# A decoder layer on one core: the ends of cross attention and of the fourth pass put in another order

## The chip, the cores and the metric

The kernel runs on one core of a Trainium2 chip. The metric is the device time of one execution in microseconds (us). A core has five engines with a program each: TensorE (PE; its weight loads are listed as PEld), VectorE (DVE), ScalarE (ACT), GpSimd (POOL) and SyncE (SP, which issues most transfers). Each runs its instructions in program order and waits on semaphores for the others.

## The reference

A decoder layer on 32 sequences of 128 rows and 128 features, in three residual parts, each on layer-normalised rows:

```python
x = x + _L0_attn_ref(_layernorm(x), W_qkv)                  # causal, one head
x = x + _L0_xattn_ref(_layernorm(x), ctx, ctx, mask, ...)   # 16 heads of 8
x = x + _L0_ffn_ref(_layernorm(x), w_gate, w_up, w_down)

def act_qdq(x):                                             # in _L0_ffn_ref
    scale = max(max(abs(x)) / 32767, 1e-12)                 # one maximum over the whole tensor
    return clip(round(x / scale), -32768, 32767) * scale
x = act_qdq(x)
up = act_qdq(x @ dequant(w_up).T)
gate = act_qdq(x @ dequant(w_gate).T)
sig = fixed_qdq_u16(sigmoid(gate))
gate = act_qdq(gate * sig)
o = act_qdq(gate * up)
return o @ dequant(w_down).T
```

Each `act_qdq` needs the largest absolute value of its whole tensor before any element can be rounded, so the feed-forward part is a row of passes over all 32 sequences with a common maximum between them.

## The kernel before

The 32 sequences (`B`) lie in eight groups (`NG`) of four (`GB`), so a group is `GT` = 512 columns wide; the hidden layer of a group has three such pieces, `FW` = 3 x `GT` = 1536 columns, and `PB` = 768 is its half. All engines' programs are written out by hand in one block each; semaphores carry the order between them, and a wait names a semaphore and the count that must be reached.

**Cross attention** runs sequence by sequence. For sequence n PE multiplies the probabilities with the values (`pv`, two halves), ScalarE copies the result out (`out_copy`), PE turns it (`queries`), VectorE divides by the sums (`attend(n)`: a reciprocal and a product), PE turns the quotient (`turn(n)`), ScalarE copies it (`turn_copy`) and PE projects it (`project(n)`). For the last three sequences VectorE adds the projection to the row (`residual`) and takes statistics (`stat3`); `aggregate3_last` closes the statistics of one or two sequences of the last group, GpSimd makes the factor of them (`roots3_last`, lines 556 to 569) and normalises two of its four sequences (line 566), VectorE the other two (`row3_last`). `largest3` takes the largest absolute value of normalised rows. PE turns the normalised rows group by group (`turn_early_rows3`, `turn_rows3`, line 630), and ScalarE or VectorE copies them (`rows3_copy`; VectorE has only group 2, line 1703). VectorE's own order at the end stands in lines 1739 to 1762, PE's in lines 948 to 985.

**The passes of the feed-forward part.** The gate (first), the up product's maximum (second), gate times sigmoid (third), and gate times up (fourth) each go over the eight groups; then the last pass multiplies by the down weights (line 1059). At the close of a pass VectorE spreads the largest value over a 128 x 128 tile (`mxw`), PE turns it (`over_partitions`, line 976), and VectorE takes the maximum over the partitions and its reciprocal (`levels_from`): the rounding of the next pass needs these.

In the **fourth pass** PE recomputes the up product of group g into PSUM (line 989), ScalarE rounds it to integers, partly into SBUF (`up_levels`, line 1344) and partly in place in PSUM (`up_levels_in_place`, line 1349), and rounds the other factor (`silu_levels`, line 1355). The product of the two is shared: GpSimd makes the first `product_split(g)` columns (lines 586 to 598) and VectorE the others (`product`, line 1891), and VectorE takes the maximum of the whole (`product_largest`, line 1820). Semaphores: `c_tn` counts the rounded gates, `c_un` the rounded ups, `c_op` GpSimd's products, `c_od` VectorE's, `c_mx` the maxima. PE fills the wait before the closing transposition with products that nobody reads (`idle_products`, line 971; two instructions each), each lot released by one of these counts (line 1049).

Of the kernel before, what the change touches and what calls it, by code (L numbers as in the profile page):

```python
# [39 lines left out]
B = 32  # L40
# [25 lines left out]
def decoder(nc, x, ctx_in, mask, Wqkv, Wq, bq, Wk, bk, Wv, bv, Wo, bo, w_gate, w_up, w_down, out):  # L66
    with ExitStack() as ctx:
# [129 lines left out]

        def product_split(g):

            return PB if g < UW or g == NG - 2 else 2 * GT  # L200

        def up_made(g):

            return g + 1 if g < UW else 2 * g - UW + 2
# [162 lines left out]
        def _(pool):  # L367
# [218 lines left out]
            for g in range(NG - 1):  # L586
# [3 lines left out]
                if g < UW:  # L590
# [2 lines left out]
                                        ).then_inc(S["c_op"], 1)  # L593
            g = NG - 1
            pool.wait_ge(S["c_tn"], NG + 1)
            pool.wait_ge(S["c_un"], up_made(NG - 2) + 2)
            nc.gpsimd.tensor_tensor(GI[:, g * FW:g * FW + GT], tn[:, g % 2, 0:GT], un[g % 3][:, 0:GT], ALU.mult
                                    ).then_inc(S["c_op"], 1)


        @block.tensor
        def _(pe):
# [176 lines left out]
            def turn(n):  # L779
                pe.wait_ge(S["t_o"], n + 1)  # L780
                pe.transpose(bank(6 + n % 2)[:, 0:P], on_[:, :], ident[:, :]).then_inc(S["t_oT"], 1)  # L781
# [167 lines left out]
                cross(n)  # L949

            queries(B - 1)
            for g in range(3):
                turn_early_rows3(g)
            turn(B - 1)
            pe.wait_ge(S["u_tca"], 1)
            turn_weights3(0, 0)
            project(B - 1)
# [88 lines left out]
                    over_partitions(4, 1)  # L1046

            pe.wait_ge(S["g_lev"], 4)
            for name, value, k in (("c_tn", NG, 6), ("c_tn", NG + 1, 4), ("c_op", NG - 1, 4), ("c_op", NG, 4), ("c_od", NG + 1, 6)):
                pe.wait_ge(S[name], value)  # L1050
                idle_products(1, k)
            over_partitions(5, 0)
# [35 lines left out]
        def _(act):  # L1088
# [251 lines left out]
            def up_levels(g, part):  # L1340
                act.wait_ge(S["c_u"], g + 1)
                wait(act, "c_op", g - 2)
                wait(act, "c_od", g - 2)
                act.activation(un[g % 3][:, part], up_bank(g)[:, part], ACT.Copy, scale=lev[:, 2:3]
                               ).then_inc(S["c_un"], 1)

            def up_levels_in_place(g, part):
                act.wait_ge(S["c_u"], g + 1)
                act.activation(up_bank(g).bitcast(I32)[:, part], up_bank(g)[:, part], ACT.Copy, scale=lev[:, 2:3]
                               ).then_inc(S["c_un"], 1)  # L1350
# [23 lines left out]
                silu_levels(g, slice(0, FW))  # L1374
            silu_levels(NG - 1, slice(0, FW))
            up_levels_in_place(NG - 1, slice(2 * GT, FW))
            up_levels(NG - 1, slice(0, GT))
            up_levels_in_place(NG - 1, slice(GT, 2 * GT))


            act.wait_ge(S["g_lev"], 5)
# [18 lines left out]
        def _(dve):  # L1400
# [256 lines left out]
            def attend(n):  # L1657
                dve.wait_ge(S["t_tr"], n + 1)
                wait(dve, "t_o", n)
                o3 = bank(6 + n % 2)[:, 2 * P:4 * P].rearrange("p (h c) -> p h c", c=VW)  # L1660
                V.reciprocal(orec[:, :], o3[:, :, DK]).then_inc(S["t_rec"], 1)
                dve.wait_ge(S["t_rec"], n + 1)
                wait(dve, "t_oT", n)
                V.tensor_tensor(on_[:, :].rearrange("p (h e) -> p h e", e=DK), o3[:, :, 0:DK],
                                bc(orec[:, :].unsqueeze(2), [P, H, DK]), ALU.mult).then_inc(S["t_o"], 1)

            def residual(n):
                dve.wait_ge(S["t_wo"], n + 1)
                x = X[:, n * P:(n + 1) * P]
                V.tensor_tensor(x, bank(6 + n % 2)[:, P:2 * P], x, ALU.add).then_inc(S["t_xd"], 1)  # L1670
# [4 lines left out]
            def stat3(n):  # L1675
                b = n % GB
                if n < B - TAIL:
                    dve.wait_ge(S["t_x2"], n + 1)
                else:
                    dve.wait_ge(S["t_xd"], n + 1 - (B - TAIL))  # L1680
                V.bn_stats(stats3(n // GB)[:, b, :], X[:, n * P:(n + 1) * P]).then_inc(S["u_stat"], 1)
# [8 lines left out]
            def aggregate3_last(b0, b1):  # L1690
                dve.wait_ge(S["u_stat"], GB * (NG - 1) + b1)
                for b in range(b0, b1):
                    m = V.bn_aggr(norms[1]["mvar"][:, 2 * b:2 * b + 2], stats3(NG - 1)[:, b, :])
                m.then_inc(S["u_agg"], 1)
# [25 lines left out]
            for n in range(B - 1):  # L1720
                g, b = divmod(n, GB)
                if n > 0:
                    attend(n - 1)
                if g > 1 and b > 1:
                    k = b - 2
                    dve.wait_ge(S["u_x3"], GB * (g - 2) + 2 * k + 2)
                    largest3(g - 2, 2 * (g - 2) + k, (2 * k, 2 * k + 2))
                if n + 3 < B:
                    maxima(n + 3, 0)
                if 1 < n < B - 1:  # L1730
                    stat3(n - 2)
                if g > 0 and b == 1:
                    aggregate3(g - 1)
                if n + 3 < B:
                    maxima(n + 3, 1)
                if n == B - 2:
                    residual(n - 1)
                    stat3(n - 1)
            aggregate3_last(0, 2)
            dve.wait_ge(S["u_x3"], GB * (NG - 2))  # L1740
            largest3(NG - 3, 2 * NG - 5, (2, 4))
            attend(B - 2)
            dve.wait_ge(S["u_x3"], GB * (NG - 1))
            largest3(NG - 2, 2 * NG - 4, (0, GB))
            residual(B - 2)
            stat3(B - 2)
            aggregate3_last(2, 3)
            attend(B - 1)
            rows3_copy(2, 2)
            dve.wait_ge(S["u_x3"], GB * (NG - 1) + 2)  # L1750
            largest3(NG - 1, 2 * NG - 3, (0, 2))
# [143 lines left out]
                largest(4, col, GI[:, g * FW + c.start:g * FW + c.stop], "c_mx")  # L1895

            for g in range(NG - 1):
                dve.wait_ge(S["c_un"], up_made(g) - (g >= UW))
                dve.wait_ge(S["c_tn"], g + 1 + (g > 0))
                product(g, slice(product_split(g), FW))  # L1900
                if g == 0:
                    V.tensor_tensor(unit[:, 4:5], scale[:, 3:4], scale[:, 2:3], ALU.mult).then_inc(S["g_unit"], 1)
                    guard_of(4)
                if g > 0:
                    dve.wait_ge(S["c_op"], g)
                    dve.wait_ge(S["c_od"], g)
                    product_largest(g - 1, g - 1, slice(0, FW))
            g = NG - 1
            dve.wait_ge(S["c_od"], NG - 1)
            product_largest(g - 1, g - 1, slice(PB, FW))  # L1910
            dve.wait_ge(S["c_op"], NG - 1)
            product_largest(g - 1, g, slice(0, PB))
            dve.wait_ge(S["c_tn"], NG + 1)
            for k, c in enumerate((slice(2 * GT, FW), slice(GT, 2 * GT))):
                dve.wait_ge(S["c_un"], up_made(NG - 2) + 1 + 2 * k)
                product(g, c)
            dve.wait_ge(S["c_op"], NG)
            dve.wait_ge(S["c_od"], NG + 1)
            product_largest(g, g + 1, slice(0, FW))
            dve.wait_ge(S["c_mx"], NG + 1)  # L1920
            dve.wait_ge(S["g_guard"], 8)
            largest_of(4, 2 * NG)
            dve.wait_ge(S["g_early"], 8)
# [72 lines left out]
```

## Time and profile before

| what | value |
|---|---|
| time before, median of three runs | 332.85 us (332.31 to 333.15) |
| profiled execution, its own time | 332.82 us |
| its span, first to last instruction | 331.0 us |
| mean granted TensorE clock | 0.995 of full speed |
| PE busy | 304.9 us, 92% |
| VectorE busy | 273.5 us, 83% |
| ScalarE busy | 255.1 us, 77% |
| GpSimd busy | 192.1 us, 58% |

All profile times are from the start of the span. The end of cross attention lies at 203 to 213 us, the end of the fourth pass at 293 to 304 us, and the last pass after it. Busy shares are averages over stages with different limits; they say nothing of either place by themselves. A line of the timeline gives start, duration, engine, source line, operation, result and operands with their shapes, the count of merged instructions, and in brackets the idle time of the engine before it and what ended that.

### The profile page before, as it was taken

How to read it: one execution, taken by the hardware profiler on the slowest of the kernel's cores; microseconds unless marked ns; L12 is line 12 of the kernel's file. 1: busy time of each engine (PE TensorE's matmuls, PEld its weight loads, DVE VectorE, ACT ScalarE, POOL GpSimd, SP SyncE). 2: the span in 40 equal slices, each digit the busy share in tenths (PEclk: the TensorE clock that was granted, in tenths of full speed). 3: DMA queues.
4: the chain of work that ended last, by engine and by line, in shares of the span. 5: the costliest groups of instructions: out<-in, count | busy, mean ns of one | idle time of the engine just before them, and what ended most of it. 6: DMA issues, size and time to landing. Idle time of an engine off the chain costs nothing.

```text
span 331.0 us, 9933 instructions
## 1 busy us (share of the span) xinstructions
PE 304.9 (92%) x3741; PEld 208.7 (63%) x3741; DVE 273.5 (83%) x652; ACT 255.1 (77%) x470; POOL 192.1 (58%) x339
## 2 busy tenths in 40 slices
PE   2899999999999999999999999999978689697996
PEld 1587877877656666666666665854423244357996
DVE  5349998878979999999999984877789996989754
ACT  3258988887789989989988987787797768993940
POOL 3467999984238698768658578200067773781000
PEclk9999999999999999999999999999997999999999
DMA  6891336672011556500000000000000000000134
GB/s 155 248 300 35 96 110 184 190 219 95 30 42 49 176 160 191 170 4 5 3 5 2 4 5 2 1 0 0 2 0 0 1 1 2 0 0 1 34 95 128
DMA packets 23755, 22.70 MB, mean 69 GB/s; under 512 B 3546, under 2 KB 21403, under 8 KB 23579
## 3 DMA queue, kind: packets, MB, share of 16 engines
q1 hardware_dynamic: 22170, 21.78, 21.4%
q8 instruction: 30, 0.49, 0.6%
q10 hardware_dynamic: 1536, 0.28, 0.5%
q14 instruction: 19, 0.15, 0.1%
HBM read 15.75 MB, written 6.31 MB: 67 GB/s over the span
## 4 chain that ended last, share of the span: by engine, by line
PE 65%; DVE 12%; ACT 8%; POOL 7%; issue 4%; DMA 2%; SPq 1%; POOLq 0%; ACTq 0%; DVEq 0%
PE banks L763 11%; PE banks L707 9%; PE banks L989 8%; DVE mxs L1820 7%; PE banks L1059 7%; PE banks L637 5%; PE banks L785 4%; PE banks L776 3%; PE banks L630 3%; ACT ng L1355 2%; PE banks L781 2%; PE banks L716 2%; POOL rstd L380 2%; PE banks L649 2%; PE banks L971 2%
## 5 line engine op out<-in xcount | busy, mean ns | idle before, releaser
L1594 DVE TENSOR_REDUCE nm<-banks 128x4 f32<-128x512 f32 x128 | 83.1, 682 | 7.2 <-PE banks L707 5.8
L1258 ACT ACTIVATE PT<-banks,bmask,vmask 128x1024 f32<-128x1024 f32 x64 | 76.6, 1199 | 0.0
L989 PE MATMUL banks<-X3T,upT 128*128 128x512 f32 x96 | 45.9, 620 | 9.9 <-DVE mxs L1820 7.3
L576 POOL TENSOR_TENSOR G<-ng,sq 128x1536 int32<-128x1536 int32 (+3 forms) x10 | 27.9, 2790 | 36.4 <-DVE sq L1851 36.4
L1820 DVE TENSOR_REDUCE mxs<-G 128x1 f32<-128x1536 int32 (+3 forms) x30 | 42.2, 1425 | 4.3 <-ACT G L1316 3.8
L763 PE MATMUL banks<-PT,VP 128*32 128x128 f32 x1024 | 41.2, 279 | 0.0
L989 PEld LDWEIGHTS banks<-X3T,upT 128*128 128x128 f32 x96 | 17.7, 196 | 33.8 <-issue 16.3
L707 PE MATMUL banks<-kd,qd 32*128 32x128 f16 x512 | 37.9, 217 | 1.1 <-ACT pT L1130 0.7
L1100 ACT ACTIVATE h<-X,shift,rstd 128x128 f32<-128x128 f32 x64 | 26.3, 483 | 10.2 <-POOL shift L425 10.1
L707 PEld LDWEIGHTS banks<-kd,qd 32*128 32x128 f16 x512 | 22.7, 92 | 17.7 <-DVE nm L1594 7.2
L763 PEld LDWEIGHTS banks<-PT,VP 128*32 128x32 f32 x1024 | 24.1, 109 | 9.8 <-issue 3.0
L380 POOL TENSOR_TENSOR rstd<-vare,mhalf 128x4 f32<-128x4 f32 (+2 forms) x26 | 25.3, 974 | 0.8
L711 PE MATMUL banks<-qd,kd 32*128 32x128 f16 x512 | 25.3, 217 | 0.1
L716 PE MATMUL banks<-mT,inj 32*128 32x128 bf16 x512 | 25.0, 215 | 0.0
L467 POOL CAST NM<-nm 128x64 bf16<-128x64 f32 x32 | 7.6, 237 | 28.8 <-DVE nm L1594 28.8
L482 POOL TENSOR_SCALAR X<-X,mvar,rstd 128x128 f32<-128x128 f32 x28 | 22.0, 793 | 0.0
L1059 PE MATMUL banks<-downT,sig 128*128 128x128 f32 x192 | 21.8, 276 | 0.0
L1059 PEld LDWEIGHTS banks<-downT,sig 128*128 128x128 f32 x192 | 21.6, 192 | 0.1
L1242 ACT ACTIVATE oT<-banks 128x128 f32<-128x128 f32 x32 | 8.9, 277 | 12.4 <-PE banks L781 12.4
L1327 ACT ACTIVATE ng<-G,lev 128x1536 int32<-128x1536 f32 (+2 forms) x9 | 12.9, 1430 | 7.0 <-POOL G L576 5.9
L989 PE MATMUL banks<-X3T,gateT 128*128 128x512 f32 x42 | 18.2, 592 | 0.0
L1316 ACT ACTIVATE G<-banks 128x512 f32<-128x512 f32 x24 | 14.0, 596 | 4.6 <-PE banks L989 3.4
(200 smaller groups left out, 744.4 us busy)
## 6 DMA issues: line engine op xcount, KB each, us to landing
kd<-k_dram SPq DMA_DIRECT2D x32, 128.0 KB, 2.7
qd<-q_dram SPq DMA_DIRECT2D x32, 128.0 KB, 2.8
ctxg<-in_ctx_dram SPq DMA_DIRECT2D x8, 256.0 KB, 3.1
X3T<-m_dram SPq DMA_DIRECT2D x1, 1792.0 KB, 10.2
out_dram<-y SPq DMA_DIRECT2D x7, 256.0 KB, 2.3
X<-in_x_dram SPq DMA_DIRECT2D x3, 512.0 KB, 10.0
k_dram<-khi SPq DMA_DIRECT2D x7, 128.0 KB, 1.9
k_dram<-klo SPq DMA_DIRECT2D x7, 128.0 KB, 1.9
```

The lines of the kernel that those rows point to most:

```text
L380: nc.gpsimd.tensor_tensor(norms[k]["rstd"][:, c], norms[k]["vare"][:, c], mhalf[:, c], ALU.pow).then_inc(S[done], 1)
L576: nc.gpsimd.tensor_tensor(GI[:, c], ng[:, u, part], sq[:, u, part], ALU.mult).then_inc(S["b_t"], 1)
L707: return pe.matmul(bank(j % 2)[:, s * P:(s + 1) * P], qd[rows(j), n // GB, s, n % GB, :], kd[rows(j), n // GB, s, n % GB, :], start=True, ...
L711: pe.matmul(bank(2 + j)[:, s * P:(s + 1) * P], kd[rows(j), n // GB, s, n % GB, :], qd[rows(j), n // GB, s, n % GB, :], start=(s == 0), sto ...
L716: return pe.matmul(bank(2 + j)[:, s * P:(s + 1) * P], inj[rows(j), s, :], mT[rows(j), n % 2, :], start=False, stop=True, skip_group_check= ...
L763: m = pe.matmul(bank(6 + n % 2)[RT * s:RT * s + RT, a * P:(a + 1) * P], VP[:, n % 2, JT * s + 2 * a + k, :], PT[:, a, (NSET * k + s) * P:( ...
L989: m = pe.matmul(bank(2 + FC * (g % 2) + k), w[:, k * P:k * P + P], grp(X3T, g), start=True, stop=True)
L1059: m = pe.matmul(bank(n)[:, b * P:(b + 1) * P], on[:, u, c * GT + b * P:c * GT + b * P + P], downT[:, c * P:(c + 1) * P], start=(c == 0), s ...
L1100: act.activation(dst[:, b_ * P:(b_ + 1) * P], seq(X, g, b_), ACT.Identity, scale=norms[k]["rstd"][:, b_:b_ + 1], bias=norms[k]["shift"][:, ...
L1258: act.activation(PT[:, a, :], bank(2 + 2 * a, 2), ACT.Exp, bias=bmask[:, n:n + 1], scale=vmask[:, n:n + 1]).then_inc(S["t_exp"], 1)
L1594: V.tensor_reduce(nm[:, n % 2, c:c + NSET], bank(u).rearrange("p (h m) -> p h m", m=P), AX.X, ALU.max, negate=True).then_inc(S["t_max"], 1)
L1820: V.tensor_reduce(mxs[:, k, col:col + 1], src, AX.X, ALU.max, apply_absolute_value=True).then_inc(S[done], 1)
```

## The change

Two places are edited together.

In the fourth pass `product_split` gives GpSimd two thirds (1024 columns) of group 6 (`NG - 2`) instead of half. Of group 7 GpSimd makes two thirds, each in an instruction of its own, where it made the first third; the second third's up levels therefore go to SBUF (`up_levels`) instead of in place. VectorE makes only the last third. VectorE's list becomes: the maximum of group 5 ahead of its product of group 6, then that product, the maximum of its third, its product of group 7, the maximum of GpSimd's two thirds of group 6, and three maxima, one for each third of group 7. PE's idle products get one more release, six after the last product of GpSimd.

In the end of cross attention VectorE scales the output of sequence 30 ahead of the aggregate of sequences 28 and 29 and two maxima, and the output of sequence 31 ahead of the statistics and the aggregate of sequence 30. PE turns the rows of group 2 after the output of sequence 31 instead of before it.

```diff
--- before.py
+++ after.py
@@ -197,7 +197,7 @@
 
         def product_split(g):
 
-            return PB if g < UW or g == NG - 2 else 2 * GT
+            return PB if g < UW else 2 * GT
 
         def up_made(g):
 
@@ -593,9 +593,10 @@
                                         ).then_inc(S["c_op"], 1)
             g = NG - 1
             pool.wait_ge(S["c_tn"], NG + 1)
-            pool.wait_ge(S["c_un"], up_made(NG - 2) + 2)
-            nc.gpsimd.tensor_tensor(GI[:, g * FW:g * FW + GT], tn[:, g % 2, 0:GT], un[g % 3][:, 0:GT], ALU.mult
-                                    ).then_inc(S["c_op"], 1)
+            for k in range(2):
+                pool.wait_ge(S["c_un"], up_made(NG - 2) + 2 + k)
+                nc.gpsimd.tensor_tensor(GI[:, g * FW + k * GT:g * FW + (k + 1) * GT], tn[:, g % 2, k * GT:(k + 1) * GT],
+                                        un[g % 3][:, k * GT:(k + 1) * GT], ALU.mult).then_inc(S["c_op"], 1)
 
 
         @block.tensor
@@ -949,9 +950,10 @@
                 cross(n)
 
             queries(B - 1)
-            for g in range(3):
+            for g in range(2):
                 turn_early_rows3(g)
             turn(B - 1)
+            turn_early_rows3(2)
             pe.wait_ge(S["u_tca"], 1)
             turn_weights3(0, 0)
             project(B - 1)
@@ -1046,7 +1048,7 @@
                     over_partitions(4, 1)
 
             pe.wait_ge(S["g_lev"], 4)
-            for name, value, k in (("c_tn", NG, 6), ("c_tn", NG + 1, 4), ("c_op", NG - 1, 4), ("c_op", NG, 4), ("c_od", NG + 1, 6)):
+            for name, value, k in (("c_tn", NG, 6), ("c_tn", NG + 1, 4), ("c_op", NG - 1, 4), ("c_od", NG, 4), ("c_op", NG, 4), ("c_op", NG + 1, 6)):
                 pe.wait_ge(S[name], value)
                 idle_products(1, k)
             over_partitions(5, 0)
@@ -1374,8 +1376,8 @@
                 silu_levels(g, slice(0, FW))
             silu_levels(NG - 1, slice(0, FW))
             up_levels_in_place(NG - 1, slice(2 * GT, FW))
-            up_levels(NG - 1, slice(0, GT))
-            up_levels_in_place(NG - 1, slice(GT, 2 * GT))
+            for k in range(2):
+                up_levels(NG - 1, slice(k * GT, (k + 1) * GT))
 
 
             act.wait_ge(S["g_lev"], 5)
@@ -1736,16 +1738,16 @@
                 if n == B - 2:
                     residual(n - 1)
                     stat3(n - 1)
+            attend(B - 2)
             aggregate3_last(0, 2)
             dve.wait_ge(S["u_x3"], GB * (NG - 2))
             largest3(NG - 3, 2 * NG - 5, (2, 4))
-            attend(B - 2)
             dve.wait_ge(S["u_x3"], GB * (NG - 1))
             largest3(NG - 2, 2 * NG - 4, (0, GB))
             residual(B - 2)
+            attend(B - 1)
             stat3(B - 2)
             aggregate3_last(2, 3)
-            attend(B - 1)
             rows3_copy(2, 2)
             dve.wait_ge(S["u_x3"], GB * (NG - 1) + 2)
             largest3(NG - 1, 2 * NG - 3, (0, 2))
@@ -1895,29 +1897,34 @@
                 largest(4, col, GI[:, g * FW + c.start:g * FW + c.stop], "c_mx")
 
             for g in range(NG - 1):
+                if g == NG - 2:
+                    dve.wait_ge(S["c_op"], g)
+                    dve.wait_ge(S["c_od"], g)
+                    product_largest(g - 1, g - 1, slice(0, FW))
                 dve.wait_ge(S["c_un"], up_made(g) - (g >= UW))
                 dve.wait_ge(S["c_tn"], g + 1 + (g > 0))
                 product(g, slice(product_split(g), FW))
                 if g == 0:
                     V.tensor_tensor(unit[:, 4:5], scale[:, 3:4], scale[:, 2:3], ALU.mult).then_inc(S["g_unit"], 1)
                     guard_of(4)
-                if g > 0:
+                if 0 < g < NG - 2:
                     dve.wait_ge(S["c_op"], g)
                     dve.wait_ge(S["c_od"], g)
                     product_largest(g - 1, g - 1, slice(0, FW))
             g = NG - 1
             dve.wait_ge(S["c_od"], NG - 1)
-            product_largest(g - 1, g - 1, slice(PB, FW))
+            product_largest(g - 1, g - 1, slice(2 * GT, FW))
+            dve.wait_ge(S["c_tn"], NG + 1)
+            dve.wait_ge(S["c_un"], up_made(NG - 2) + 1)
+            product(g, slice(2 * GT, FW))
             dve.wait_ge(S["c_op"], NG - 1)
-            product_largest(g - 1, g, slice(0, PB))
-            dve.wait_ge(S["c_tn"], NG + 1)
-            for k, c in enumerate((slice(2 * GT, FW), slice(GT, 2 * GT))):
-                dve.wait_ge(S["c_un"], up_made(NG - 2) + 1 + 2 * k)
-                product(g, c)
-            dve.wait_ge(S["c_op"], NG)
-            dve.wait_ge(S["c_od"], NG + 1)
-            product_largest(g, g + 1, slice(0, FW))
-            dve.wait_ge(S["c_mx"], NG + 1)
+            product_largest(g - 1, g, slice(0, 2 * GT))
+            dve.wait_ge(S["c_od"], NG)
+            product_largest(g, g + 1, slice(2 * GT, FW))
+            for k in range(2):
+                dve.wait_ge(S["c_op"], NG + k)
+                product_largest(g, g + 2 + k, slice(k * GT, (k + 1) * GT))
+            dve.wait_ge(S["c_mx"], NG + 3)
             dve.wait_ge(S["g_guard"], 8)
             largest_of(4, 2 * NG)
             dve.wait_ge(S["g_early"], 8)
```

## Rows read from the trace of the kernel before

**Rows 1.** Chain of work that ended last: start, us, what; the two closing transpositions.

```profile
212.78 0.30 PE banks L976
...
304.20 0.33 PE banks L976
```

**Rows 2.** Timeline of VectorE, end of cross attention.

```profile
204.26 0.29 DVE L1681 BATCH_NORM_STATS2 stats<-X 128x6 f32<-128x128 f32 x1
...
205.06 0.25 DVE L1661 RECIPROCAL orec<-banks 128x16 f32<-128x16 f32 x1
205.34 0.29 DVE L1664 TENSOR_TENSOR on_<-banks,orec 128x128 f32<-128x128 f32 x1
...
207.80 0.24 DVE L1661 RECIPROCAL orec<-banks 128x16 f32<-128x16 f32 x1
...
208.88 0.69 DVE L1703 COPY X3T<-banks 128x512 f32<-128x512 f32 x1 [0.52 <-PE banks L630]
...
209.84 0.29 DVE L1670 TENSOR_TENSOR X<-banks,X 128x128 f32<-128x128 f32 x1
```

**Rows 3.** Timeline of PE, the same stretch.

```profile
204.18 0.41 PE L776 MATMUL banks<-ident,oun 128*128 128x128 f32 x2 [0.28 <-ACT oun L1237]
...
205.69 0.33 PE L781 MATMUL banks<-ident,on_ 128*128 128x128 f32 x1 [0.52 <-DVE on_ L1664]
...
207.10 0.44 PE L776 MATMUL banks<-ident,oun 128*128 128x128 f32 x2
207.37 1.47 PE L630 MATMUL banks<-ident,X 128*128 128x128 f32 x12
208.68 0.27 PE L781 MATMUL banks<-ident,on_ 128*128 128x128 f32 x1
...
209.32 0.49 PE L785 MATMUL banks<-WXT,oT 128*128 128x128 f32 x2
```

**Rows 4.** Timeline of GpSimd, the same stretch: two sequences of group 7 normalised.

```profile
206.03 1.57 POOL L566 TENSOR_SCALAR X<-X,mvar,rstd 128x128 f32<-128x128 f32 x2
```

**Rows 5.** Timeline of VectorE, end of the fourth pass.

```profile
293.85 1.75 DVE L1820 TENSOR_REDUCE mxs<-G 128x1 f32<-128x1536 int32 x1
296.29 0.95 DVE L1891 TENSOR_TENSOR G<-ng,banks 128x768 int32<-128x768 int32 x1 [0.70 <-ACT ng L1355]
...
300.54 1.28 DVE L1891 TENSOR_TENSOR G<-ng,banks 128x512 int32<-128x512 int32 x2
301.92 1.75 DVE L1820 TENSOR_REDUCE mxs<-G 128x1 f32<-128x1536 int32 x1
```

**Rows 6.** Timeline of GpSimd and ScalarE, end of the fourth pass.

```profile
293.22 2.37 POOL L592 TENSOR_TENSOR G<-ng,unx 128x1024 int32<-128x1024 int32 x1 [0.33 <-ACT ng L1355]
...
296.26 1.82 POOL L592 TENSOR_TENSOR G<-ng,X 128x768 int32<-128x768 int32 x1 [0.67 <-ACT ng L1355]
...
298.66 0.70 ACT L1349 ACTIVATE banks<-banks,lev 128x512 int32<-128x512 f32 x1
298.95 1.27 POOL L597 TENSOR_TENSOR G<-ng,X 128x512 int32<-128x512 int32 x1 [0.86 <-ACT X L1344]
```

**Rows 7.** VectorE's groups by line and shape: count, busy us, mean ns, idle before.

```profile
L1820 DVE TENSOR_REDUCE mxs<-G 128x1 f32<-128x512 f32 x6 | 3.8, 677 | 0.2 <-ACT G L1316 0.2
...
L1891 DVE TENSOR_TENSOR G<-ng,banks 128x512 int32<-128x512 int32 x5 | 3.3, 682 | 0.7 <-ACT ng L1355 0.7
L1891 DVE TENSOR_TENSOR G<-ng,X 128x768 int32<-128x768 int32 x2 | 2.5, 1228 | 2.4 <-ACT ng L1355 2.4
```

**Rows 8.** Timeline of PE, the last idle products before the transposition at 304.20.

```profile
301.88 1.60 PE L971 MATMUL banks<-ident 128*128 128x128 f32 x12 [0.45 <-DVE G L1891]
```

**Rows 9.** Timeline of PE in the third pass, and one stretch's busy times with granted clock.

```profile
241.98 5.42 PE L989 MATMUL banks<-X3T,upT 128*128 128x512 f32 x12 [0.84 <-DVE mxs L1820]
249.47 7.23 PE L989 MATMUL banks<-X3T,upT 128*128 128x512 f32 x12 [2.07 <-DVE mxs L1820]
...
251.00:252.00 1.00, 1.00 (x2) 0.34 (x1) 1.00 (x1) 0.97 (x2) 1.00 (x1) 0.50 0.00 0
```

## The prediction, made before the change was run

> **What bounds the kernel now.** I read the profile from the outside in. The chain of waits comes first, because it names the work that ended last. Its steps at the two edited places are VectorE and PE work, and each place closes with a transposition on PE that gathers one maximum over the partitions: at 212.78 for the levels of the normalised rows, and at 304.20 for the levels of the product [rows 1]. Nothing of the next pass can begin before its transposition, so time saved ahead of one is saved for the whole kernel, and time saved beside it is lost. The question at each place is therefore when the transposition's input is ready.
>
> Then I read the timeline of each engine ahead of both points, since shares of the span say nothing of a place 8 us long. In the end of cross attention the reader is to see that VectorE does statistics and maxima that nobody waits for yet, while PE waits for the scaled output of sequence 30: the product starts at 205.34 and PE's transposition only at 205.69, though the input (two transpositions of 0.41 from 204.18) was ready at 204.59 [rows 2, 3]. In the end of the fourth pass the reader is to see VectorE idle for 0.70 before 296.29, waiting for ScalarE, and then never idle until 303.67 [rows 5]; GpSimd ends its last product at 298.95 + 1.27 = 300.22 and does nothing more [rows 6]. So VectorE alone sets this end.
>
> **The change, part 1: the end of the fourth pass.** Counted from 295.6, VectorE's list is rebuilt. Group 7's middle third goes to GpSimd, and so does a sixth of group 6; the whole maximum of group 5 moves ahead of group 6's product, into the idle 0.70. One reduce more is issued in all: eight instructions where there were seven.
>
> Steps between starts: two independent 512-wide products with an operand in PSUM take 1.28 together, at a mean of 0.682 each, so an instruction that waits for nothing starts 0.08 before its predecessor ends [rows 5, 7]. One that waits for its predecessor's own result starts 0.10 after it (300.54 + 1.28 = 301.82, then 301.92) [rows 5]. A reduce of 512 costs 0.677 [rows 7], one of 1536 costs 1.75 [rows 5]; 1024 lies half way, an estimate of 1.21.
>
> The maximum of group 5 needs GpSimd's product of group 5, done at 293.22 + 2.37 = 295.59 [rows 6], and VectorE, free at 293.85 + 1.75 = 295.60 [rows 5]. With 0.04 for the signal it starts at 295.64. Then: group 6's third at 297.31; its maximum, which waits for it, at 298.09; group 7's third at 298.69; the maximum of group 6's two thirds at 299.29; group 7's three maxima at 300.42, 301.02 and 301.62. From the start of the last reduce to the transposition it was 304.20 - 301.92 = 2.28 with 1536 wide [rows 1, 5]; with 512 it is 2.28 - (1.75 - 0.68) = 1.21. VectorE is ready for the transposition at 302.83, a gain of 1.37.
>
> The others must keep up. GpSimd: group 6 now takes 2.37 instead of 1.82, so 296.26 to 298.63, still before the 298.95 at which ScalarE's levels let group 7 begin [rows 6]; nothing is queued late. The second third of group 7 needs ScalarE's last levels, done at 298.66 + 0.70 = 299.36 [rows 6], and follows at 300.22, done at 301.49. The last reduce at 301.62 is thus only 0.1 behind it. ScalarE: group 6's levels change from 768 + 768 to 512 + 1024 columns, and the last 512 go to SBUF instead of PSUM; equal width, and I cost it at nothing. It hides under GpSimd's 1.27, and if it ran late by more than 0.86 it would show.
>
> PE is the third that must keep up. Its idle products before the transposition are in program order, and the last six now wait for GpSimd's last product. In the trace the six are twelve instructions of 1.60 in all [rows 8]; a successor overlaps such a run by 0.16 (208.84 against 208.68) [rows 3], so the transposition comes about 1.44 behind their start, or nearer 1.34 if no gap lies ahead of them. From 301.54 this gives 302.9 to 303.0. PE's own fillers, not VectorE, are then last, by about 0.1. I take 302.9: a gain of **1.3**. Bounds: 1.4 (VectorE gates) and 0.6 (the GpSimd rival below).
>
> **Part 2: the end of cross attention.** Scaling output 30 moves ahead of an aggregate and two maxima; VectorE is free at 204.26 + 0.29 = 204.55 [rows 2]. The reciprocal starts when its input is done, at 204.62 instead of 205.06; the product follows 0.28 later, as in the trace, and everything behind it on PE and ScalarE up to the transposition of output 31 comes 0.43 earlier: PE's transposition at 205.26, the two of output 31 at 206.67 instead of 207.10, done at 207.11 [rows 3]. Output 31 is now scaled ahead of the statistics of 30: reciprocal at 207.14 instead of 207.80 [rows 2], product done at 207.71.
>
> PE in the meantime turns eight blocks of rows from 206.94, 0.109 each [rows 3], and is free at 207.81, just when the scaled output arrives (207.77). It is turned at 207.81 instead of 208.68. The four blocks of group 2, moved behind it, end at about 208.52 instead of 208.84 [rows 3]; VectorE's copy of them, which waited 0.52 for PE, starts at 208.56 instead of 208.88 [rows 2]. From there VectorE's list to the transposition at 212.78 is unchanged and almost without a gap, and what it needs is there: the last projection is ready for VectorE at 209.2 (ScalarE's copies come earlier by the same shift) where VectorE reaches it at 209.52; before, these two tied (209.32 + 0.49 = 209.81 against a start at 209.84) [rows 2, 3]. The gain is **0.32**. The moved statistics reach GpSimd later, the first of them by about what scaling output 30 takes, 0.53 with its step; its rows of group 7 end at 206.03 + 1.57 + 0.53 = 208.13 instead of 207.60 [rows 4], a microsecond before their maximum at 209.17, so I cost this at nothing. If that cover were gone, up to the whole 0.32 would be. Bounds: 0, and 0.43, the whole shift ahead of the copy.
>
> **The sum.** The profiled execution took 332.82, its span 331.0 and 1.8 around it, and agrees with the median of 332.85. 332.82 - 1.3 - 0.32 = **331.2**.
>
> **The rivals.**
> *Cross attention gives nothing.* GpSimd's later factors, or PE's reordered turns, end as late as before. For it: many signals from engine to engine lie in 4 us, and PE and the scaled output tie at 207.8. Against it: the margins above. Time: 332.82 - 1.3 = 331.5.
>
> *GpSimd becomes the bound of the fourth pass.* Its last product runs at 1.27 only in one row, alone against VectorE's reduces. A VectorE product with both operands in SBUF took 1.23 on average beside GpSimd's products, against 0.95 for the one with an operand in PSUM [rows 5, 7]: sharing exists. If both of GpSimd's last products stretched by 1.23/0.95 = 1.29, they would end at 298.95 + 2 x 1.64 = 302.23, PE's transposition would come at 303.6, and the gain would be 0.6: 331.9. Against it: VectorE's new instructions beside them are reduces and products with an operand in PSUM, and GpSimd's 2.37 at 293.22 lies beside just these [rows 5, 6]. The Trainium skill, page GPSIMD Engine Reference, section Specifications, says the same: contention arises with VectorE instructions that have two SBUF inputs or use a two-port mode. By that rule the stretch would be nil and this case vanishes; the trace agrees as far as it goes, so its chance is small.
>
> *Slower: PE's clock falls.* Twelve matmuls of the third pass took 7.23 at 249.47 against 5.42 at 241.98; PE had been idle for 2.07 before, and the granted clock in 251 to 252 is 0.50, the lower level of 1.2 GHz [rows 9]. One such fall in the last pass, which is PE's, costs 1.8 and turns the forecast into 332.82 - 1.62 + 1.8 = 333.0, slower than before; it decides from a fall of 1.6 on. For it: the stretch ahead is idle products, whose times all move. Against it: their gaps shrink, the six new ones fill the hole that lay behind GpSimd's last product, and a stretch with 0.45 of idle ahead of the last fillers [rows 8] kept its clock. The Trainium skill, page TensorE: Matmul & The Clock Gate, section Part 1, says that the throttled state is the default and that activity releases it; by that rule fewer idle moments can only help, which the two rows of the third pass bear out.
>
> **How the numbers follow.** Forecast 0.70, nothing from cross attention 0.12, GpSimd bound 0.09, clock 0.04, others 0.05. Runs of this kernel spread by 0.3% (1.0 us), which is also what a measurement can tell from no change, so faster means below 331.85. Of the forecast 0.95 lies there, of the second case 0.8, of the third 0.45: together 0.80. Slower by over 0.3% is half of the clock case and a part of the others: 0.03; the rest, 0.17, is no difference. The range goes from both upper bounds, 332.82 - 1.42 - 0.43 = 331.0 less half the spread, 330.5, to the GpSimd case with some of the spread, 332.3.
>
> **What would show it.** In the changed profile: group 5's maximum on VectorE at 295.6 less 0.3, with no idle before the product of group 6; the last reduce 512 wide and within 0.2 of the end of GpSimd's last product; PE's fillers running into the last transposition; the copy of group 2's turned rows 0.3 earlier. I am wrong if VectorE waits for GpSimd ahead of one of its last two reduces by more than 0.2, if the 212.78 transposition has not moved, or if the last pass shows a granted clock below 1.

## The result, and the profile after

The changed kernel takes 330.55 us (median of 7 runs, 329.86 to 331.62) against 332.63 for the kernel before in the same comparison (332.07 to 333.28, 7 runs). The ratio is 0.9945 with a 95% interval of 0.9932 to 0.9958, so 1.4 to 2.3 us faster. The difference of the two medians, 2.08, lies in that interval. The profiled execution took 331.25 with a span of 329.5; against the profiled 332.82 of before that is 1.57 less.

Two stretches measure the two parts by themselves, free of whatever moved ahead of them. For cross attention it runs from the start of VectorE's addition of sequence 29's projection (the operation of `residual`) to the closing transposition; for the fourth pass from the start of ScalarE's rounding of group 6's gate (`silu_levels`) to the closing transposition.

| stretch, us | before | after | gain |
|---|---|---|---|
| end of cross attention | 212.78 - 203.94 = 8.84 | 212.51 - 204.00 = 8.51 | 0.33 |
| between the two | 294.59 - 212.78 = 81.81 | 294.33 - 212.51 = 81.82 | 0 |
| end of the fourth pass | 304.20 - 294.59 = 9.61 | 302.69 - 294.33 = 8.36 | 1.25 |

The lines that the table rests on, beside those of [rows 1]: first the three of before, then the four of after. The last line of each is VectorE's reading of the second transposition.

```profile
203.94 0.29 DVE L1670 TENSOR_TENSOR X<-banks,X 128x128 f32<-128x128 f32 x1 [1.82 <-PE banks L785]
294.59 3.06 ACT L1355 ACTIVATE ng<-G,lev 128x1536 int32<-128x1536 int32 x2
304.57 0.29 DVE L1773 TENSOR_REDUCE step<-banks 128x1 f32<-128x128 f32 x1 [0.42 <-PE banks L976]
...
204.00 0.29 DVE L1672 TENSOR_TENSOR X<-banks,X 128x128 f32<-128x128 f32 x1 [1.82 <-PE banks L786]
212.51 0.30 PE L978 MATMUL banks<-ident,mxw 128*128 128x128 f32 x1 [0.94 <-DVE mxw L1769]
294.33 3.06 ACT L1357 ACTIVATE ng<-G,lev 128x1536 int32<-128x1536 int32 x2
303.00 0.29 DVE L1775 TENSOR_REDUCE step<-banks 128x1 f32<-128x128 f32 x1 [0.59 <-PE banks L978]
```

Counted to that reading, the fourth pass gains a little more than to the start of the transposition: 304.57 - 294.59 = 9.98 before and 303.00 - 294.33 = 8.67 after, so 1.31. The transposition takes 0.33 after a wait [rows 1] and 0.27 right behind other matmuls, as below.

The timeline of VectorE in the end of the fourth pass, after (start, duration, engine, line, operation, operands, count):

```profile
293.59 3.53 DVE L1822 TENSOR_REDUCE mxs<-G 128x1 f32<-128x1536 int32 x2
297.04 0.68 DVE L1893 TENSOR_TENSOR G<-ng,banks 128x512 int32<-128x512 int32 x1
297.75 0.69 DVE L1822 TENSOR_REDUCE mxs<-G 128x1 f32<-128x512 int32 x1
298.35 0.68 DVE L1893 TENSOR_TENSOR G<-ng,banks 128x512 int32<-128x512 int32 x1
298.95 2.99 DVE L1822 TENSOR_REDUCE mxs<-G 128x1 f32<-128x1024 int32 x4
301.97 0.17 DVE L1712 TENSOR_REDUCE mx<-mxs 128x1 f32<-128x16 f32 x1
302.18 0.23 DVE L1931 TENSOR_SCALAR mxw<-mx 128x128 f32<-128x128 f32 x1
```

Where [rows 5] had 0.70 of idle time and a product of 768, no idle time is shown any more: the two maxima of 1536 run into each other, the product of 512 follows, and the last four maxima form one block. The spread maximum is ready at 302.18 + 0.23 = 302.41. PE and GpSimd in the same stretch:

```profile
296.07 6.78 PE L973 MATMUL banks<-ident 128*128 128x128 f32 x56 [0.59 <-ACT ng L1357]
302.69 0.27 PE L978 MATMUL banks<-ident,mxw 128*128 128x128 f32 x1
302.80 2.17 PE L973 MATMUL banks<-ident 128*128 128x128 f32 x18
...
296.00 2.36 POOL L592 TENSOR_TENSOR G<-ng,X 128x1024 int32<-128x1024 int32 x1 [0.67 <-ACT ng L1357]
298.69 2.51 POOL L598 TENSOR_TENSOR G<-ng,X 128x512 int32<-128x512 int32 x2 [0.32 <-ACT X L1346]
```

PE's 56 idle instructions stand in one row without a wait up to the transposition, which carries no idle time and no releaser and comes 0.28 after its input was made. That it waited for PE's own queue is tested below. Before, the idle products were over at 301.88 + 1.60 = 303.48 [rows 8], well ahead of the transposition at 304.20 [rows 1]. GpSimd ends at 298.69 + 2.51 = 301.20. VectorE's last maximum, one of 0.68 that ends with its block at 301.94, starts at about 301.26, only 0.06 later, so GpSimd is the next to become last.

The end of cross attention after, VectorE first and then PE, to be read against [rows 2, 3]:

```profile
204.69 0.26 DVE L1663 RECIPROCAL orec<-banks 128x16 f32<-128x16 f32 x1
204.98 0.29 DVE L1666 TENSOR_TENSOR on_<-banks,orec 128x128 f32<-128x128 f32 x1
...
208.66 0.69 DVE L1705 COPY X3T<-banks 128x512 f32<-128x512 f32 x1 [0.45 <-PE banks L631]
209.26 0.41 DVE L1708 TENSOR_REDUCE mxs<-X 128x1 f32<-128x256 f32 x1
...
205.33 0.33 PE L782 MATMUL banks<-ident,on_ 128*128 128x128 f32 x1
...
207.88 0.30 PE L782 MATMUL banks<-ident,on_ 128*128 128x128 f32 x1
208.02 0.60 PE L631 MATMUL banks<-ident,X 128*128 128x128 f32 x4
...
208.78 0.39 PE L786 MATMUL banks<-WXT,oT 128*128 128x128 f32 x2
```

The whole stretch lies 0.06 later in this execution. Output 30 is turned at 205.33 without a wait shown (0.52 before), output 31 at 207.88 instead of 208.68, and VectorE's copy starts at 208.66 instead of 208.88.

### The profile page after: what moved, and what is told of

Its sections match the earlier page's. It is cut to its first block, busy times and chain, and to the rows that moved or that the text cites. A ratio compares the mean times of both kernels' runs of the same rounds, so it can differ in the third digit from the quotient of the medians.

```text
span 329.5 us, 9951 instructions
## 1 busy us (share of the span) xinstructions
PE 301.7 (92%) x3749; PEld 206.7 (63%) x3749; DVE 272.4 (83%) x653; ACT 255.1 (77%) x470; POOL 193.9 (59%) x340
## 3 DMA queue, kind: packets, MB, share of 16 engines
q10 hardware_dynamic: 1536, 0.28, 0.5%
## 4 chain that ended last, share of the span: by engine, by line
PE 62%; DVE 10%; ACT 8%; POOL 8%; issue 4%; DMA 4%; SPq 2%; POOLq 0%; ACTq 0%; DVEq 0%
PE banks L764 11%; PE banks L708 9%; PE banks L991 8%; PE banks L1061 7%; DVE mxs L1822 6%; PE banks L786 4%; PE banks L973 4%; PE banks L638 3%; PE banks L777 3%; PE banks L782 3%; PE banks L717 2%; ACT ng L1357 2%; POOL rstd L380 2%; PE banks L631 2%; POOL pickd L399 2%
## 5 line engine op out<-in xcount | busy, mean ns | idle before, releaser
L991 PE MATMUL banks<-X3T,upT 128*128 128x512 f32 x96 | 44.3, 601 | 11.4 <-DVE mxs L1822 8.9
L1822 DVE TENSOR_REDUCE mxs<-G 128x1 f32<-128x1536 int32 (+5 forms) x32 | 42.4, 1345 | 4.2 <-ACT G L1318 3.8
```

Of the source, the lines that this page charges most:

```text
L991: m = pe.matmul(bank(2 + FC * (g % 2) + k), w[:, k * P:k * P + P], grp(X3T, g), start=True, stop=True)
L1822: V.tensor_reduce(mxs[:, k, col:col + 1], src, AX.X, ALU.max, apply_absolute_value=True).then_inc(S[done], 1)
```

## The experiments

All stretches below are the two defined above. The theory: the two places add; in the fourth pass the filled wait and the smaller share of VectorE each carry a part until PE's idle products take over as the bound; in cross attention VectorE's two moves carry the gain and PE's move gives some back. The rivals: one edit does it all, the added instructions eat what they save, or the clock has a part in it.

**Each place alone.** The cross attention edits undone, and the fourth pass edits undone, with the change otherwise whole.

> The change without its cross attention part. If the two places are independent, as the theory has it, the stretch from the start of ScalarE's rounding of group 6's gate to the closing transposition of the fourth pass is 8.36 us as in the changed kernel (9.61 before), the stretch from the addition of sequence 29's projection to the closing transposition of cross attention is 8.84 as before, and the time falls by about 1.25. If instead the changed kernel's larger difference of medians (2.1 where its trace shows 1.5 to 1.6) is a gain of this part, by the clock or otherwise, the time falls by about 1.8.

Measured: fourth pass 302.31 - 293.94 = 8.37, cross attention 212.12 - 203.28 = 8.84, time 330.9 against 332.29, ratio 0.9961 (0.9947 to 0.9975), which is 1.3 us.

> The change without its fourth pass part. Theory: the stretch from the addition of sequence 29's projection to the closing transposition is 8.51 as in the changed kernel (8.84 before), all passes behind it keep their lengths, and the time falls by 0.3, which timing alone can hardly tell from nothing. The rival that this part gives nothing has 8.84. The rival that it carries the rest of the difference of medians has 0.8.

Measured: cross attention 212.23 - 203.71 = 8.52, fourth pass 303.65 - 294.05 = 9.60, the stretch between 81.82; time 332.23 against 332.29, ratio 0.9999 (0.9990 to 1.0008). The trace shows 0.32 at its place; the time can't tell it from nothing, and its interval just reaches it. The places are independent, as the theory has it. A gain of 0.8 from cross attention, the rival's, is ruled out. The 1.8 that the other rival gives the fourth pass lies at the very edge of the interval (0.8 to 1.8 us); it is unlikely and not excluded by the time.

**The order alone in the fourth pass.**

```diff
             for g in range(NG - 1):
+                if g == NG - 2:
+                    dve.wait_ge(S["c_op"], g)
+                    dve.wait_ge(S["c_od"], g)
+                    product_largest(g - 1, g - 1, slice(0, FW))
...
-                if g > 0:
+                if 0 < g < NG - 2:
```

> The kernel before with one edit: the maximum of group 5 moved ahead of VectorE's product of group 6; all splits as before. Theory: it fills VectorE's idle 0.70 ahead of that product, and nothing else moves, so the stretch from ScalarE's rounding of group 6's gate to the transposition falls from 9.61 to about 8.95, just over half of the part's 1.25. The rival that the gain is all in the smaller share of VectorE has it at 9.61, with the idle time moved behind the maximum.

Measured: 303.09 - 294.03 = 9.06, a gain of 0.55 where 0.66 was expected. The idle 0.70 is gone:

```profile
293.29 3.52 DVE L1820 TENSOR_REDUCE mxs<-G 128x1 f32<-128x1536 int32 x2
296.73 0.94 DVE L1891 TENSOR_TENSOR G<-ng,banks 128x768 int32<-128x768 int32 x1
297.70 1.81 DVE L1820 TENSOR_REDUCE mxs<-G 128x1 f32<-128x768 int32 x2
```

The missing 0.1 is in the second step: with the maximum of group 5 no longer between them, group 6's product and its maximum follow each other directly, and the maximum waits for the product's own result (297.67 to 297.70) instead of starting 0.08 before the end of its predecessor.

**The splits alone.** The same edit undone in the changed fourth pass, with cross attention as before.

> The fourth pass with the new splits (two thirds of groups 6 and 7 on GpSimd, maxima by thirds, the added idle products), but with the maximum of group 5 still behind VectorE's product of group 6, and cross attention as before. Theory: VectorE's list ends where its work from 296.29 on ends: 0.6 from the product to the maximum, 1.67, then as in the changed kernel, about 0.6 to 0.65 later than there. VectorE gates again, not PE's idle products, so the stretch is about 8.75 to 8.8 (8.36 in the changed kernel, 9.61 before). If the added instructions cost what the smaller share saves, it is 9.6.

Measured: 302.70 - 294.04 = 8.66, a gain of 0.95, slightly more than expected. Here each of VectorE's instructions starts before its predecessor ends, so none waits for its predecessor's result:

```profile
295.73 0.69 DVE L1892 TENSOR_TENSOR G<-ng,banks 128x512 int32<-128x512 int32 x1 [0.70 <-ACT ng L1356]
296.34 2.34 DVE L1821 TENSOR_REDUCE mxs<-G 128x1 f32<-128x1536 int32 x2
298.59 0.68 DVE L1892 TENSOR_TENSOR G<-ng,banks 128x512 int32<-128x512 int32 x1
299.19 2.99 DVE L1821 TENSOR_REDUCE mxs<-G 128x1 f32<-128x1024 int32 x4
```

The new splits, their maxima and the added release went in together here, so their shares in the 0.95 are not known. 0.55 + 0.95 = 1.50 is more than the 1.25 of both together, so something else takes over when both are there.

**What takes over.** The six idle products behind GpSimd's last product become four.

```diff
-... ("c_op", NG, 4), ("c_op", NG + 1, 6)):
+... ("c_op", NG, 4), ("c_op", NG + 1, 4)):
```

> The changed kernel with four idle products instead of six behind GpSimd's last product. Theory: in the changed kernel VectorE's spread maximum is ready at 302.41 but PE turns it only at 302.69, because the twelve idle instructions are still in its queue; with eight PE is free 0.45 earlier and VectorE gates, so the stretch from ScalarE's rounding of group 6's gate to the transposition falls from 8.36 to 8.12 to 8.15, and the granted clock of the last pass stays 1. If the transposition waited for VectorE after all, it stays at 8.36.

Measured: 301.53 - 293.40 = 8.13. VectorE's spread maximum is made at 301.25 + 0.23 = 301.48, PE turns it 0.05 later, and the mean granted clock of the span is 1.000:

```profile
301.25 0.23 DVE L1931 TENSOR_SCALAR mxw<-mx 128x128 f32<-128x128 f32 x1
...
295.14 6.33 PE L973 MATMUL banks<-ident 128*128 128x128 f32 x52 [0.60 <-ACT ng L1357]
301.53 0.33 PE L978 MATMUL banks<-ident,mxw 128*128 128x128 f32 x1
```

The gain of the place is then 9.61 - 8.13 = 1.48, the 1.50 of the two edits by themselves. The idle products took 0.23 of it. Part comes back at once: with four, the transposition stands behind a wait and takes 0.33 instead of 0.27, and VectorE reads it 301.89 - 293.40 = 8.49 behind the start of the stretch (8.67 in the changed kernel). Net, the two extra idle products cost 0.18.

**The clock.** All idle products ahead of the closing transposition of the fourth pass taken away (the nine behind it remain).

```diff
                 pe.wait_ge(S[name], value)
-                idle_products(1, k)
```

> The changed kernel without any of the idle products ahead of the closing transposition of the fourth pass (the nine behind it remain). It tests the clock rival and its price: PE is then idle for some 7 us. Theory: the transposition comes 0.2 to 0.25 earlier, as with four idle products, but the granted clock falls to 0.5 (1.2 GHz) and the last pass begins at it: 1.8 or more longer, by the twelve matmuls that took 7.23 instead of 5.42 in the third pass of the kernel before. If the clock did not care, the time is 0.2 below the changed kernel's.

Measured: the transposition comes at 8.21, 0.15 earlier than in the changed kernel instead of 0.2 to 0.25, because it starts 0.14 after its input (302.75) where it was 0.05 with four idle products, and the last pass loses far more. PE was idle for 7.07 ahead of it:

```profile
302.89 0.45 PE L978 MATMUL banks<-ident,mxw 128*128 128x128 f32 x1 [7.07 <-DVE mxw L1930]
303.13 4.05 PE L973 MATMUL banks<-ident 128*128 128x128 f32 x18
```

The stretches of 1 us behind it (us, PE, weight loads, VectorE, ScalarE, GpSimd, granted clock, DMA share, GB/s):

```profile
304.00:305.00 1.00, 1.00 (x6) 1.00 (x6) 0.96 (x3) 1.00 (x3) 0.00 (x0) 0.50 0.00 0
...
308.00:309.00 1.00, 1.00 (x8) 1.00 (x7) 0.01 (x1) 1.00 (x2) 0.00 (x0) 0.63 0.00 0
309.00:310.00 1.00, 1.00 (x11) 1.00 (x11) 0.00 (x0) 1.00 (x2) 0.00 (x0) 1.00 0.00 0
```

The granted clock is 0.50, which is 1.2 GHz, until past 308. The eighteen idle instructions take 4.05 instead of 2.17, the last pass's matmuls start 4.08 behind the transposition instead of 2.12, and they take 22.46 in all instead of 21.80. Net: 1.96 + 0.66 - 0.15 = 2.5 us slower than the changed kernel's trace, and the execution took 334.07 against 333.05 for the kernel before. The clock rival had its mechanism right and its price of 1.8 too low: the fall cost 1.96 + 0.66 = 2.6. The Trainium skill, page TensorE: Matmul & The Clock Gate, section Part 1, has the throttled state as the default that activity releases; the trace agrees, at 0.50 behind 7.07 of idle time and 1.00 again after the busy stretch behind it.

**PE's order in cross attention.** The change with PE's move undone (the edit shown), and the kernel before with PE's move alone (the same lines the other way round).

```diff
-            for g in range(2):
+            for g in range(3):
                 turn_early_rows3(g)
             turn(B - 1)
-            turn_early_rows3(2)
```

> The changed kernel with PE's order of cross attention as before (the rows of group 2 turned ahead of the last output). Theory: VectorE's two moves alone carry the gain and PE's move takes some of it back: the copy of group 2's rows no longer stands behind the last output and starts 0.1 earlier than in the changed kernel, the projection of the last output comes later but just in time, and the stretch from the addition of sequence 29's projection to the transposition is 8.40 to 8.45 (8.51 in the changed kernel, 8.84 before). Rival: the last projection becomes the bound and the stretch is 8.55 to 8.7.

Measured: 211.99 - 203.56 = 8.43. The copy starts 208.08 - 203.56 = 4.52 after the stretch's start (4.66 in the changed kernel, 4.94 before), and the last projection comes just in time:

```profile
208.08 0.69 DVE L1704 COPY X3T<-banks 128x512 f32<-128x512 f32 x1 [0.31 <-PE banks L631]
208.69 0.41 DVE L1707 TENSOR_REDUCE mxs<-X 128x1 f32<-128x256 f32 x1
209.05 0.29 DVE L1671 TENSOR_TENSOR X<-banks,X 128x128 f32<-128x128 f32 x1
...
208.52 0.49 PE L786 MATMUL banks<-WXT,oT 128*128 128x128 f32 x2
```

It ends at 209.01 and its addition starts at 209.05. This tie costs a little: from the copy to the transposition VectorE's list takes 211.99 - 208.08 = 3.91, as before the change (212.78 - 208.88 = 3.90), and 212.51 - 208.66 = 3.85 in the changed kernel, where the projection is early. So PE's move delays the copy by 0.14 and gains 0.06 behind it.

> The kernel before with PE's move alone (the last output turned ahead of the rows of group 2). Theory: without VectorE's moves the last output is scaled late, PE waits for it with the rows of group 2 behind it, and the copy of these comes about 0.2 to 0.25 later: the stretch from the addition of sequence 29's projection to the transposition grows from 8.84 to about 9.05 to 9.1. Rival: PE's move helps by itself through an earlier projection, 8.7 or less.

Measured: 212.88 - 203.74 = 9.14, 0.30 worse than before and a little more than expected. The rows of group 2 stand behind an output that is scaled late, and VectorE waits 0.86 for them:

```profile
209.03 0.69 DVE L1704 COPY X3T<-banks 128x512 f32<-128x512 f32 x1 [0.86 <-PE banks L630]
```

So of the part's three edits VectorE's two carry 8.84 - 8.43 = 0.41, and PE's takes 0.08 back; without them it would cost 0.30. VectorE's two were not tried apart. The sizes are from one trace each; the same code in another trace repeats them to 0.01 or 0.02 (8.51, 8.52 and 8.51; 8.43 and 8.42).

**The surplus of the medians, and a better version.** The change once more beside a version with PE's order undone, four idle products instead of six behind GpSimd's last product, and seven instead of nine behind the transposition. Of its edit only the last part is new:

```diff
             over_partitions(5, 0)
-            idle_products(1, 9)
+            idle_products(1, 7)
```

> The changed kernel once more, on a chip with the next one. By the traces the two places give 1.58 us, a ratio of 0.9953; the first comparison gave 0.9945 with 0.9932 to 0.9958. If the surplus is scatter of the first 82 us, ahead of both places (the first maximum of cross attention starts between 81.4 and 82.8 us in the traces so far), this comparison comes nearer to 0.9953, and the stretch between the two places stays as it was. If it is a gain that the traces miss, it stays at 0.9945 or below.

Measured: 331.06 against 332.66, ratio 0.9941 (0.9921 to 0.9962); stretches 8.51, 81.82 and 8.34. The ratio did not come nearer to 0.9953, though both intervals hold that value. It is not the quotient of the two medians: these are 1.60 us apart, 0.9952, where those of the first comparison were 2.08 apart, 0.9937. So whether there is a surplus at all depends on how the same runs are summed up. What the traces do show is the scatter ahead of both places. The first maximum of cross attention on VectorE, in the run with four idle products and in this one:

```profile
81.42 1.29 DVE L1596 TENSOR_REDUCE nm<-banks 128x4 f32<-128x512 f32 x2 [0.28 <-PE banks L708]
...
82.95 1.29 DVE L1596 TENSOR_REDUCE nm<-banks 128x4 f32<-128x512 f32 x2
```

The program is the same up to there, and the two differ by 1.53, as much as the change is worth. The ratios stand for 1.8 to 2.0 us against 1.58 in the traces; whether any of these 0.2 to 0.4 us is more than scatter stays open, but for the 0.05 behind the transposition that the stretches leave out.

> A version built from the findings: the changed kernel with PE's order of cross attention as before, four idle products instead of six behind GpSimd's last product, and seven instead of nine behind the closing transposition. Theory: 0.08 in cross attention (8.43 instead of 8.51), 0.23 ahead of the transposition (8.13 instead of 8.36), and about 0.2 behind it, where the first piece for the last pass is ready at 303.42 but PE starts on it at 303.70 (in the run with four idle products): 0.5 in all below the changed kernel, 2.1 below the kernel before, 0.9937, if the granted clock stays 1 in the last pass. If the fewer idle products let the clock fall there, it is 1.8 or more slower.

Measured: 330.60 against 332.66, ratio 0.9940 (0.9926 to 0.9954): faster than the kernel before, not told apart from the change by time. In the trace cross attention takes 8.42 and the fourth pass 8.13, as expected. The seven idle products brought nothing. The first matmul of the last pass comes 2.04 behind the transposition instead of 2.17 with nine, but the pass's matmuls then take 21.94 instead of 21.80; the granted clock of the last pass stayed at 1. From the start of the first stretch to the end of the last pass's matmuls it takes 122.35 where the changed kernel takes 122.61, so it is 0.26 better than the change where it was meant to be 0.5: 0.05 of the 0.23 comes back at the transposition, and the 0.2 behind it was not there.

## Why the prediction was right

**The sum.** Forecast 1.3 + 0.32 = 1.62; the traces show 1.25 + 0.33 = 1.58. The 1.57 between the profiled executions confirms this only in part: the changed one started the first stretch 0.06 later and gained another 0.05 behind the last transposition, and the two cancel. The predicted 331.2 is the profiled 331.25. That the time agrees so well is partly luck: the median is 330.55, only just above the lower end of the range, 330.5, in a comparison whose seven executions of the changed kernel lie up to 1.8 us apart. The interval of the ratio holds 1.58. In the forecast's list "one reduce more" should be two more and one product less; its count of eight instructions is right.

**The fourth pass, step by step.** The changed trace lies 0.26 earlier by then (294.33 against 294.59). With that taken off, the forecast had the product of group 6 at 297.05 (measured 297.04), its maximum at 297.83 (297.75), group 7's product at 298.43 (298.35), the block of the last four maxima at 299.03 (298.95) and the transposition at 302.64 (302.69). The one step off is the wait for an own result, which cost 0.03 behind the end instead of 0.10; it makes most of the 0.1 by which VectorE's list ended earlier than forecast. The forecast's upper bound of 1.4 for the case that VectorE gates is too low for it: the run with four idle products has 1.48.

**Which engine is last.** The forecast put PE's own idle products ahead of VectorE by about 0.1; it was 0.23, and the run with four of them shows that by taking it back. GpSimd kept up as reckoned: 1.27 for each of its last two products, done at 301.20, forecast 301.49 - 0.26 = 301.23.

**The GpSimd rival** did not occur: its two last products took 2.51 together, beside VectorE's maxima and a product with an operand in PSUM. The Trainium skill, page GPSIMD Engine Reference, section Specifications, names contention with VectorE instructions that have two SBUF inputs or use a two-port mode, and the trace agrees: beside VectorE instructions with at most one SBUF input the two kept the 1.27 of before. The rows of the kernel before also show that the rival had the wrong engine lengthened. Its 1.23 is an average of unlike cases, VectorE products of 768 with two SBUF inputs:

```profile
279.71 0.96 DVE L1891 TENSOR_TENSOR G<-ng,X 128x768 int32<-128x768 int32 x1 [1.52 <-ACT ng L1355]
281.97 1.50 DVE L1891 TENSOR_TENSOR G<-ng,X 128x768 int32<-128x768 int32 x1 [0.84 <-ACT ng L1355]
285.05 1.21 DVE L1891 TENSOR_TENSOR G<-ng,unx 128x768 int32<-128x768 int32 x1
...
280.84 1.81 POOL L592 TENSOR_TENSOR G<-ng,X 128x768 int32<-128x768 int32 x1 [4.99 <-DVE G L1891]
283.64 1.81 POOL L592 TENSOR_TENSOR G<-ng,X 128x768 int32<-128x768 int32 x1 [0.99 <-DVE G L1891]
```

With no GpSimd product beside it VectorE's took 0.96, and 1.50 and 1.21 where it overlapped one for 0.68 and 0.40. GpSimd's took 1.81 in both overlaps, no longer than the 1.82 beside a reduce and a product with an operand in PSUM [rows 6].

**Cross attention.** Its size was right to 0.01, and that is partly luck. The mechanism named gave less than forecast: the copy of group 2's rows came 0.28 earlier against the stretch's start, not 0.32. The other 0.05 came from VectorE's list behind the copy, which the forecast called unchanged: the last projection no longer ties with its addition there. GpSimd's moved factors did no harm. What I did not ask is whether all three edits help. The same rows would have told it: without PE's move the copy would have followed twelve transpositions from 206.94, at 208.45 instead of 208.56. The runs show the copy 0.14 earlier and the stretch 0.08 shorter.

**The clock rival** did not occur: the granted clock from 300 to 302.6 and in the last pass is 1.00:

```profile
300.00:302.60 2.60, 2.60 (x25) 2.53 (x24) 2.34 (x6) 0.00 (x0) 1.19 (x1) 1.00 0.00 0
306.00:329.50 23.50, 20.61 (x183) 20.29 (x182) 13.21 (x20) 10.38 (x10) 0.00 (x0) 1.00 0.30 91
```

Its mechanism exists, and the run without idle products shows what guards the change from it.

## What to carry to other kernels

When an engine sets the end of a stage, fill its waits with work whose inputs are already there, then move work to an engine that ends earlier, and reckon both in steps between starts; after each step ask who is last now, fillers included. Matmuls that only keep PE's clock up, ahead of a critical instruction, must fit between the last release and the instruction's input, since they stand in the same queue: here two products too many cost 0.18, and none at all 2.5. Where a change joins several edits, weigh each by itself: one of the three in cross attention cost a quarter of what the part gained.

## What the runs showed of the hardware

A fall of the granted clock in the third pass cost nothing. Before, twelve matmuls took 7.23 behind 2.07 of idle time [rows 9]; after, the same work behind the same idle time kept its clock, 1.00 in 251 to 252:

```profile
249.19 2.84 PE L991 MATMUL banks<-X3T,upT 128*128 128x512 f32 x6 [2.07 <-DVE mxs L1822]
253.53 2.84 PE L991 MATMUL banks<-X3T,upT 128*128 128x512 f32 x6 [1.49 <-DVE mxs L1822]
```

The stretch between the two places was 81.81 with the fall and 81.82 without it, because VectorE's maxima set that pass; at full clock PE waits 1.49 for them instead. The fall came there in seven of the twelve traces. In three others, that of the changed kernel among them, the granted clock was 0.50 from 20 to 23 us instead, and in two (fourth pass with new splits alone, and four idle products) it stayed at 1.00 until the last pass was done. So the same gap may or may not bring the clock down, and the price depends on whether PE sets the stage: nothing there, 2.5 us in the last pass. The other surprise is the scatter of the first 82 us, 1.5 us between executions of the same instructions. The clock does not settle it: in the three traces with the early fall the first maximum of cross attention starts at 82.3 to 83.0, in the other nine at 81.4 to 82.8. Its cause stays open.
